# A decoder layer on one core: prepared weight pieces of 1528 columns that skip every fourth unit

## The reference, cut to what matters

```python
x = x + attention(layernorm(x))        # 16 heads of 128, soft-capped by tanh, causal, gated per head, then w_out
x = x + token_experts(layernorm(x))    # expert = token id // 6250, 4 of them; g = u = the same 512x512 matrix ctx[e]
x = x + moe(layernorm(x))              # 8 routed experts of width 352, best two per token, and a shared one of width 704
```

## Time and profile before

| | us |
|---|---|
| median of 3 runs | 1718.95 |
| lowest, highest | 1718.5, 1726.83 |
| the profiled execution | 1730.75 |
| its span | 1729.0 |
| mean granted clock of TensorE in it | 0.978 |

### The profile page before, as it was taken

One profiled execution on the slowest core, in us unless ns is written; L12 is line 12 of the kernel. 1 busy time (PEld: TensorE's weight loads), 2 busy tenths in 40 slices (PEclk: granted clock), 3 DMA queues, 4 the chain that ended last, 5 costly groups with the idle time before them and its releaser, 6 DMA issues.

```text
span 1729.0 us, 25231 instructions
## 1 busy us (share of the span) xinstructions
PE 1659.6 (96%) x8576; PEld 1431.7 (83%) x8577; DVE 887.8 (51%) x1523; ACT 589.1 (34%) x1036; POOL 716.1 (41%) x610
## 2 busy tenths in 40 slices
PE   7999999999999999999999999998999999999996
PEld 6888888888888888888878877787998888998895
DVE  4787656676665775656665665334524222222221
ACT  4444443334333333443333333331221112232231
POOL 4666554564544563544554542001202302333342
PEclk9999999999999999999999999999779999999998
DMA  8776456677577577577678673632600015777753
GB/s 290 289 281 221 139 202 210 224 282 260 196 255 264 208 278 257 184 265 256 215 272 309 215 295 134 215 108 74 238 6 19 19 23 172 212 245 226 220 94 43
DMA packets 93710, 342.07 MB, mean 198 GB/s; under 512 B 15053, under 2 KB 15092, under 8 KB 87988
## 3 DMA queue, kind: packets, MB, share of 16 engines
q1 hardware_dynamic: 79572, 303.10, 48.9%
q0 software_dynamic: 14048, 37.79, 9.2%
HBM read 220.86 MB, written 120.00 MB: 197 GB/s over the span
## 4 chain that ended last, share of the span: by engine, by line
PE 59%; DMA 14%; POOL 11%; issue 10%; DVE 3%; ACT 2%; SPq 0%; POOLq 0%; DVEq 0%; ACTq 0%
PE bank L314 18%; PE bank L316 17%; PE bank L315 17%; DMA pre_raw<-pre 7%; DMA out<-rows,ids_e 7%; POOL pre_split L528 4%; POOL key_sums L579 2%; POOL probs L569 2%; PE bank L1588 2%; POOL key_sums L577 1%; PE bank L1561 1%; PE bank L1644 1%; POOL key_sums L575 1%; PE bank L1463 1%; PE bank L1634 1%
## 5 line engine op out<-in xcount | busy, mean ns | idle before, releaser
L569 POOL TENSOR_TENSOR probs<-probs,causal 128x256 f32<-128x256 f32 x126 | 91.4, 746 | 414.4 <-ACT probs L763 414.4
L316 PE MATMUL bank<-store,wqk 128*128 128x512 f32 x512 | 202.1, 395 | 0.0
L315 PE MATMUL bank<-store,wqk 128*128 128x512 f32 x512 | 201.9, 394 | 0.0
L314 PE MATMUL bank<-store,wqk 128*128 128x512 f32 x512 | 201.9, 394 | 0.0
L1078 DVE SCALAR_TENSOR_TENSOR resid<-bank,factor,resid 128x512 f32<-128x512 f32 x256 | 189.3, 741 | 14.7 <-PE bank L316 14.6
L1072 DVE TENSOR_TENSOR q_lo<-bank,q_hi 128x512 fp32r<-128x512 f32 x64 | 44.3, 692 | 192.9 <-ACT q_hi L803 192.9
L761 ACT ACTIVATE probs<-bank 128x512 f32<-128x512 f32 x189 | 85.8, 528 | 157.2 <-PE bank L316 157.2
L858 ACT ACTIVATE act_sb<-bank 128x352 f32<-128x352 f32 (+1 forms) x90 | 42.7, 492 | 262.0 <-PE bank L316 262.0
L1246 DVE TENSOR_TENSOR aT_lo<-bank,aT_hi 64x128 fp32r<-64x128 f32 (+3 forms) x145 | 54.4, 416 | 144.7 <-ACT aT_hi L849 142.6
L528 POOL TENSOR_TENSOR pre_split<-pre_raw,pre_split 128x1152 fp32r<-128x1152 f32 x45 | 120.3, 2673 | 12.1 <-ACT pre_split L724 12.1
L314 PE MATMUL bank<-wo,o_hi 128*128 128x512 f32 x256 | 107.0, 418 | 16.9 <-DVE resid L1078 15.7
(11 more groups left out here) (268 smaller groups left out, 4345.9 us busy)
## 6 DMA issues: line engine op xcount, KB each, us to landing
pre_parts<-pre_split SPq DMA_DIRECT2D x45, 1152.0 KB, 5.5
wqk<-wqk_parts SPq DMA_DIRECT2D x96, 512.0 KB, 3.4
pre_raw<-pre SPq DMA_DIRECT2D x45, 576.0 KB, 7.0
store<-wv_parts SPq DMA_DIRECT2D x12, 2048.0 KB, 9.6
wo<-wo_parts SPq DMA_DIRECT2D x48, 512.0 KB, 6.5
expert_w<-pre_parts SPq DMA_DIRECT2D x8, 2816.0 KB, 13.0
wqk_parts<-wqk SPq DMA_DIRECT2D x16, 1024.0 KB, 5.4
expert_w<-pre_parts SPq DMA_DIRECT2D x8, 1536.0 KB, 8.9
```

Source lines behind the costliest of these rows:

```text
L314: nc.tensor.matmul(out_ap, a_hi, b_hi, start=first, stop=False)
L315: nc.tensor.matmul(out_ap, a_hi, b_lo, start=False, stop=False)
L316: return nc.tensor.matmul(out_ap, a_lo, b_hi, start=False, stop=last)
L569: nc.gpsimd.tensor_tensor(diagonal, diagonal, causal[:, :, :], ALU.mult).then_inc(S["masked"], 1)
```

## The change

Pieces are made only in units whose number doesn't leave 1 when divided by four, from unit 18 on: 18, 19, 20, 22, 23, 24, ... 58, 59, 60, 62, which are 34 units. The pieces have 1528 columns. A unit asks whether the next one has a piece (`following`) and issues its load if so, behind its own store if it has one. Thus the load for the unit behind a skipped one is issued in the skipped one. `pre_split` now reaches over `zeros`, which is last used in unit 7. Six small tensors move to the region of the third stage's routing, so that the tiles behind them lie some 1 KB lower. `PRE_COLS`, the row pitch of the prepared weights in HBM, goes from 51,840 to 51,952 columns. Cut to its core:

```diff
-PRE_JOBS, PRE_JOB = 45, 1152
+PRE_JOBS, PRE_JOB = 34, 1528
...
-        meta_all = sb("meta_all", [P, ETILES, 2])
-        ids_e = sb("ids_e", [P, ETILES], U32)
...
+        meta_all = sb("meta_all", [P, ETILES, 2])
+        ids_e = sb("ids_e", [P, ETILES], U32)
...
-        assert sb_pre.at <= sb.at
+        assert sb_pre.at <= nc.sbuf_usable_end
...
-        PRE_SLOT = HEADS + 1
+        PRE_SLOTS = [u for u in range(HEADS + 2, U) if u % TB != 1][:PRE_JOBS]
         CT_JOBS = -(-CT_COLS // PRE_JOB)
+
+        def pre_job(u):
+
+            return PRE_SLOTS.index(u) if u in PRE_SLOTS else None
...
-                j = u - PRE_SLOT
-                if j == -1:
-                    load_pre(0)
-                if 0 <= j < PRE_JOBS:
+                j, following = pre_job(u), pre_job(u + 1)
+                if j is not None:
                     sp.wait_ge(S["pre_lo"], j + 1)
                     sp.dma_start(pre_parts[:, :, j * PRE_JOB:(j + 1) * PRE_JOB], plain(pre_split[:, :, :])).then_inc(S["pre_stored"], 16)
-                    if j + 1 < PRE_JOBS:
-                        load_pre(j + 1)
+                if following is not None:
+                    load_pre(following)
...
-                if 0 <= u - PRE_SLOT < PRE_JOBS:
-                    low_pre(u - PRE_SLOT)
+                if pre_job(u) is not None:
+                    low_pre(pre_job(u))
...
-                if 0 <= u - PRE_SLOT < PRE_JOBS:
-                    high_pre(u - PRE_SLOT)
+                if pre_job(u) is not None:
+                    high_pre(pre_job(u))
```

More of the change, by code:

```diff
@@ L171, in build @@
         row_sum = sb("row_sum", [P, TILES])
+        meta_all = sb("meta_all", [P, ETILES, 2])
+        ids_e = sb("ids_e", [P, ETILES], U32)
+        expert_e = sb("expert_e", [P, ETILES], I32)
+        loads_e = sb("loads_e", [P, ETILES], I32)
+        place_e = sb("place_e", [P, ETILES], I32)
+        expert_end = sb("expert_end", [P, EXPERTS], I32)
         assert sb.at <= weights_at
```

## The result

The four runs of the changed kernel beside four of the kernel before give medians of 1704.95 and 1720.84 us, a ratio of 0.9891 with a 95% interval of 0.9849 to 0.9933. Six more beside eleven on one chip give 1701.74 and 1721.42, 0.9885 (0.9855 to 0.9915): 19.7 us, 1.1% faster. The profiled execution took 1705.89 us (span 1704.2) against 1730.75.

A forecast was written before the change was run, and what follows sets the result against it. TensorE, busy 96% of the span, bounds the kernel, with ten gaps behind late piece loads. Removing them, -23.3 us, plus 7 us in ordinary units sums to -16.3 us: 1702.7 us from a median of 1718.95, range 1694 to 1717.

The forecast's parts named there:

- Removed, -23.3 us: Ten stalled units 21 to 57: without the piece, k_hi follows q_hi directly and they fall to their neighbours' length, -23.3 us.
- The clock's dips go with the gaps: Units 33, 41, 53, clock 0.91, last some 2 us more than the other seven; these dips go too, within -23.3 us.
- The limit of 4.53 us behind q_hi, one for one: ScalarE in ordinary units: k_hi can begin some 4.53 us behind q_hi at no cost; beyond that, cost is one for one.
- V's weights next, 2.7 us of cover: Skipped units: V's weights land at 610.3, V's product would ask at 613.0; 2.7 us of cover, so no wait.
- Rival D: The ten units stall on V's weights once the piece is gone, keeping 10 of the 23.3 us: 1713 us; chance 0.06.
- +7 us in the ordinary units: 22 pieces loaded behind the previous unit's store: eight slow landings make k_hi 1.00 us late each, together taken as +7 us.
- +1.85 to +2.3 us. I take +2.1: Later landing of ordinary units' loads from 564 KB more in store and load, by slopes of 3.3 to 4.0 us per 1000 KB.
- the forecast's own formula: Ordinary units' cost for landing growth x: 14 (x - 2.44) where x exceeds 2.44, plus 8 (x - 1.10).
- The forecast's own signs of this cost: Ordinary units: loads behind a store land after 8.4 us, a third near 9.7; resid waits about 7 us in eight units.
- The last piece and the moved tensors, 0: Last piece moves from unit 61 to 62, small tensors to other addresses: 0 each, each bounded by +2 us.
- rival C: Full gain: x is 1.85 or slow landings fall on skipped units; 23 us won, 1696 us; chance 0.18.
- a growth x of 1.85: What the larger store and load add to a landing in ordinary units, at the low end, a condition for the full gain.

The follow-up runs named there:

- before, k_hi first: Kernel before (45 pieces of 1152 columns, none skipped) with ScalarE's k_hi ahead of its copy of the piece: 1702.66 us, ratio 0.9888 to the kernel before.
- size alone: Changed kernel's 34 pieces of 1528 columns, one in each unit from 17 to 50, none skipped: 1734.20 us in one run.
- V's weights last: Kernel before with the issue of V's weights moved behind the piece's store and load in units that are multiples of four: 1713.06 us in one run.
- extra store: Changed kernel with a second store of each piece's high half (764 KB) ahead of the next load: 1734.77 us in one run.

## Why the prediction was right, and where not

The forecast was 1702.7 us; the first four runs gave 1704.95 and the next six 1701.74, both well within 1694 to 1717, and faster by more than 0.5%.

- *Removed, -23.3 us*: shown, as -23.1. The ten units fell from 177.49 to 154.43 us, to the length of their neighbours (154.30); "before, k_hi first" shows that it was the place of k_hi, "size alone" that it was not the number of pieces.
- *The clock's dips go with the gaps*: shown in this stretch. Each dip in the two traces of before adds 1.5 to 1.6 us to its unit beyond the gap, and unit 53 of the second trace, with the lowest clock (0.84), has 2.8. In the two traces of the changed kernel every unit from 17 to 62 has a clock of 1.00. What a dip is can be read in unit 33 of the first trace of before: the granted clock is 0.50 from 554 to 556 us, and matmuls of 128x512 begin 0.43 us apart there (553.71, 554.13, 554.56, 554.99) against 0.23 in unit 35 at a clock of 1.00. No row gives the clock in GHz: the forecast's 1.2 and 2.4 are an estimate, and 512 columns in 0.427 us at half the clock, which is 1.2 columns per ns, agree with it if TensorE takes a column a cycle.
- *The limit of 4.53 us behind q_hi, one for one*: right as a mechanism; measured 4.62. The recorded working doesn't give 4.53 either: 598.3 - 593.72 is 4.58, 0.04 from the measured limit.
- *V's weights next, 2.7 us of cover*: right, they were not waited for, and "V's weights last" shows what stands behind that cover: issued somewhat later they stall seven units. Rival D is out.
- *+7 us in the ordinary units*: **this term was wrong; it measures 0.2**. The step that failed is "+1.85 to +2.3 us. I take +2.1": both slopes were taken from single transfers' times to landing at different sizes, and the measured growth is 1.3 to 1.5 us for 564 KB, 2.3 to 2.7 for 1000 KB. With 1.4 the forecast's own formula gives 8 x (1.4 - 1.10) = 2.4 us, and with 4.62 for 4.53 and a copy of 1.49 for 1.55 about 1. The rest is the count. Only four units have k_hi beyond 4.62 us, 23, 35, 39 and 55, each behind a long landing, and they lose 0.01 to 0.12 us. Of the other four the load of unit 47 is long no more (7.8 us), and in 24, 27 and 44 k_hi begins at 4.21, 4.44 and 4.15: the first of these loads took 8.6 us and not 9.0, and the other two were issued in units that last some 15.77 us, which leaves them more time. The forecast's own signs of this cost, landings of 8.4 and near 9.7 us and some 7 us of waits for resid in eight ordinary units, did not come: the landings are near 7.7 and 9.0, and TensorE waits for no resid.
- *The last piece and the moved tensors, 0*: units 61 and 62 last as before (13.99 and 13.45 for 14.00 and 13.45 us), and TensorE's waits behind them are of the same kinds and lengths as before.
- *The sum*: rival C, the full gain, is what happened up to unit 63 (22.9 us). The forecast gave as its condition a growth x of 1.85, but by its own formula that still costs 6 us; it was the growth of 1.4, and the shorter list of late units, that brought it. The median moved by only 15.9 in the first runs, and so the forecast of 16.3 hit the number with 7 us of cost that doesn't exist: that closeness is luck. The next group's 19.7 is nearer to what was won.
- *The rest, 19.7 for 22.9*: open. No loss by the change is shown: the later stages differ by 9.2 us between two executions of the same changed kernel. One thing on record speaks for the traces showing more than the median execution lost. The two traced executions of the kernel before (1730.75 and 1730.16) lie 8 to 12 us above its medians, and the dips in the ten units cost 4.7 and 5.9 us in them, so that without any dip the ten units would have lost 18 to 19 us (an estimate from these traces). How many dips the untraced executions had is not known. Of the eleven in the first group the fastest (1715.1) has the highest mean clock, 0.984; that of the slowest (1730.63) is 0.978.

## What to carry to other kernels

When an engine runs a list in order, look at what stands behind each wait for a DMA: here a copy that nobody needed soon stood ahead of one that TensorE needed within 4.6 us, and putting the urgent one first made the late load all but free, at no cost in size or layout. Before enlarging a transfer to make fewer of them, compute where its landing falls against that limit; here 1.7 us more to landing (the medians) and 0.6 us more to issue, in the extra store, took back 21.4 of the 23 us in the ordinary units, and with a late wqk half behind it all of the gain and some 8 us more. And where runs scatter by more than the effect, compare the time at which a certain unit starts in the trace.

## What the hardware showed that was not expected

- The time to landing of a load that follows a store grew by only 1.3 to 1.5 us for 564 KB more in the two, less than from 512 to 1152 KB (2.1 us for 640 KB) between different transfers.
- The slow landings are not scattered at random. In both kernels the loads issued in units 22, 23, 26, 34, 38, 43 and 54 are the long ones (7.4 to 7.9 us before, 8.6 to 9.2 changed). In the kernel before, five of the eight long ones have a 16 KB packet of the queue that the profile calls q8 instruction between their issue and their landing, and none of the fourteen quick ones has; in the changed kernel it is four of seven and one of fifteen. That these packets are the cause isn't shown: three long loads have none in either kernel.
- A gap of TensorE in these units doesn't always bring a lower clock. In the first trace of the kernel before TensorE waits 1.9 us in unit 33 and the unit's clock is 0.91; in the second it waits 1.9 us in unit 41 and the clock stays at 1.00:

```profile
552.81 0.50 PE L314 MATMUL bank<-wo,o_hi 128*128 128x512 f32 x1 [1.90 <-DVE resid L1078]
```

```profile
682.93 0.50 PE L314 MATMUL bank<-wo,o_hi 128*128 128x512 f32 x1 [1.91 <-DVE resid L1078]
```

- The later stages of an unchanged program vary: of two traces of the changed kernel the 140 us from 1150 on have a granted clock of 0.82 in one and 0.87 in the other, as these windows show (first the trace with 1704.2 us of span, then the one with 1695.6):

```profile
1150.00:1290.00 140.00, 129.55 (x690) 120.62 (x690) 66.61 (x213) 26.74 (x57) 18.47 (x17) 0.82 0.26 95
```

```profile
1150.00:1290.00 140.00, 129.78 (x725) 119.72 (x724) 67.61 (x217) 28.55 (x62) 20.59 (x19) 0.87 0.27 95
```

By an estimate from these two rows, the 0.05 of clock over 140 us is 7 us at full clock, so most of the 9.2 us between the two. Why the lower clock lasted longer in one of them is open.
